# A post-norm layer (sparse attention, gated network) on one core: the down product moved into the next batch's slots, gate and up spread, a constant matrix pass taken out

## The reference, cut to what matters

```python
Q, K, V = proj(Wq, bq), proj(Wk, bk), proj(Wv, bv)          # (16, 16 heads, 512, 16)
scores = einsum('bhqd,bhkd->bhqk', Q, K) / sqrt(16)
thresh = top_k(scores, 31)[0][..., -1:]
attn = softmax(where(scores < thresh, -inf, scores))
x = layernorm(x + (attn @ V) @ Wo.T + bo)
g, u = x @ (w_gate / 127).T, x @ (w_up / 127).T              # int weights, hidden 768
x = layernorm(x + (silu(g) * u) @ (w_down / 127).T)
```

## Time and profile before

| what | value |
|---|---|
| median of 3 runs | 2992.36 us (2987.83 to 2993.67) |
| profiled execution | 3002.92 us, span 3001.1 us |
| PE busy | 2705.3 us (90%) |
| DVE busy | 2499.2 us (83%) |
| ACT busy | 2478.7 us (83%) |
| POOL busy | 2385.7 us (79%) |
| mean granted TensorE clock | 0.959 of full speed |

### The profile page before, as it was taken

One profiled execution on the slowest core, in us unless ns is written; L12 is line 12 of the kernel. 1 busy time (PEld: TensorE's weight loads), 2 busy tenths in 40 slices (PEclk: granted clock), 3 DMA queues, 4 the chain that ended last, 5 costly groups with the idle time before them and its releaser, 6 DMA issues.

```text
span 3001.1 us, 81706 instructions
## 1 busy us (share of the span) xinstructions
PE 2705.3 (90%) x21375; PEld 1449.9 (48%) x21375; DVE 2499.2 (83%) x12312; ACT 2478.7 (83%) x5890; POOL 2385.7 (79%) x1668
## 2 busy tenths in 40 slices
PE   5889999989998988899999999999988999899897
PEld 2444544545454444454545455454444545455455
DVE  5888888888889878888898988878888888888883
ACT  4888898888898877888888988878978888888883
POOL 1887888888798876787888888787877879778783
PEclk7899999999999989899999999999999999999998
DMA  3201111020111101111011110211101111110100
GB/s 88 48 21 42 25 41 38 24 49 26 37 30 36 42 21 37 29 29 45 23 42 25 41 39 24 47 27 37 30 25 45 26 40 27 32 42 23 37 2 22
DMA packets 91162, 102.67 MB, mean 34 GB/s; under 512 B 34529, under 2 KB 52962, under 8 KB 90594
## 3 DMA queue, kind: packets, MB, share of 16 engines
q1 hardware_dynamic: 89874, 96.35, 13.4%
q10 hardware_dynamic: 720, 0.14, 0.0%
HBM read 20.86 MB, written 8.39 MB: 10 GB/s over the span
## 4 chain that ended last, share of the span: by engine, by line
PE 36%; DVE 18%; SPq 15%; issue 13%; POOL 8%; ACT 6%; DMA 2%; DVEq 1%; ACTq 0%; POOLq 0%
SPq L386 8%; SPq L385 7%; DVE cand L941 7%; POOL mask L1219 6%; PE bench L740 5%; PE Y_ps L664 5%; PE ST_ps L684 4%; PE Y_ps L661 3%; PE ctxT_ps L698 3%; DVE S L934 3%; PE bench L734 3%; PE bench L605 3%; PE Y_ps L662 3%; PE ST_ps L681 3%; ACT junk L492 2%
## 5 line engine op out<-in xcount | busy, mean ns | idle before, releaser
L1219 POOL TENSOR_SCALAR mask<-S,thr,mb 128x512 bf16<-128x512 f32 x1015 | 2098.4, 2080 | 44.1 <-POOL mb L1213 33.5
L941 DVE MAX8 cand<-Y_ps 128x8 f32<-128x128 f32 x4096 | 1072.0, 282 | 7.4 <-issue 6.9
L492 ACT ACTIVATE junk<-S,at_zero,slope 128x512 bf16<-128x512 f32 x1024 | 824.7, 805 | 99.3 <-DVE S L934 99.2
L934 DVE TENSOR_SCALAR_CACHE_REDUCE S<-S_ps,na 128x512 f32<-128x512 f32 x1024 | 755.9, 738 | 170.7 <-PE S_ps L651 153.2
L502 ACT ACTIVATE above<-S,s,steep 128x512 bf16<-128x512 f32 x1024 | 824.6, 805 | 0.6
L510 ACT ACTIVATE PT<-ST_ps 128x512 f32<-128x512 f32 x1024 | 595.9, 582 | 193.0 <-PE ST_ps L684 187.4
L661 PE MATMUL Y_ps<-ones_b,nbig 128*128 128x512 bf16 x1024 | 403.0, 394 | 169.6 <-DVE cand L941 155.9
L651 PE MATMUL S_ps<-KS,QS 64*128 64x512 f32 x1024 | 523.0, 511 | 4.5 <-DVE S L934 2.3
L664 PE MATMUL Y_ps<-KS,QS 64*128 64x512 f32 x1024 | 523.0, 511 | 0.0
L684 PEld LDWEIGHTS ST_ps<-nbig,mask 128*128 128x128 bf16 x4096 | 235.8, 99 | 382.0 <-issue 382.0
L684 PE MATMUL ST_ps<-nbig,mask 128*128 128x128 bf16 x4096 | 414.8, 225 | 0.0
(11 more groups left out here) (187 smaller groups left out, 3684.6 us busy)
## 6 DMA issues: line engine op xcount, KB each, us to landing
QS<-Qhi SPq DMA_DIRECT2D x512, 32.0 KB, 2.0
KS<-Khi SPq DMA_DIRECT2D x512, 32.0 KB, 2.0
KS<-Klo SPq DMA_DIRECT2D x512, 32.0 KB, 2.0
QS<-Qlo SPq DMA_DIRECT2D x512, 32.0 KB, 2.0
xTs<-in_xT SPq DMA_DIRECT2D x17, 512.0 KB, 3.7
xs<-in_x SPq DMA_DIRECT2D x16, 512.0 KB, 3.9
out<-xs SPq DMA_DIRECT2D x15, 512.0 KB, 2.9
hT<-in_wgT SPq DMA_DIRECT2D x1, 768.0 KB
```

The costliest lines, as they stand in the source:

```text
L492: nc.scalar.activation(junk[:, :], S[:, score_place(j)[0], :], ACT.Tanh, bias=at_zero[:, :], scale=slope[:, hb, col:col + 1], accum_out=s0 ...
L934: nc.vector.tensor_scalar(S[:, at, :], S_ps[n % 2][:, :], na[:, hb, col:col + 1], None, ALU.add, op1=ALU.max, accum_out=rmax[:, n % RING:n ...
L941: mx = nc.vector.max(cand[:, j % CANDS, i, :], Y_ps[j % 2][:, i * BW:(i + 1) * BW])
L1219: nc.gpsimd.tensor_scalar(mask[:, h % MASKS, t, :], S[:, score_place(j)[0], :], thr[:, r:r + 1], mb[:, r:r + 1], ALU.is_lt, op1=ALU.add).t ...
```

## The change

- Scores are made small: the K weights and bias are multiplied once by `SHIFT` (2^-38), the exponential undoes it, `BIG` falls from 2^40 to 4.
- `count_second` writes its sign as an unsigned byte into the upper byte of each bf16 of `above` (the lower bytes stay 0). A negative sign gives 0, a positive one a tiny bf16, and one product with `nbyte` (-2^127 on the diagonal) pushes the flagged scores down. The product of `nbig` with ones (line 661) is gone.
- The flags and `onesc` are bf16.
- Gate and up move to slots 43/44, 46/47, 49/50, 52/53, 58/59, 61/62; the second half's gram, quad and sums from 36, 37, 55 to 42, 45, 54.
- The down product moves from slots 59 to 62 to slots 1, 2, 3, 5 of the next batch; the second layer norm to slot 7 on POOL, 10 and 12 on ACT.
- Batch 1, which has no down product, is unrolled; the loops start at batch 2, with 7 batches in the body for PE, ACT and POOL and 2 for DVE.

```diff
-BIG = 2.0 ** 40
+SHIFT = 2.0 ** -38
+BIG = 4.0
+BYTE_BIG = 2.0 ** 127
-             26: "v", 31: "q", 33: "k", 35: "keys", 36: "gram", 37: "quad", 55: "sums"}
+             26: "v", 31: "q", 33: "k", 35: "keys", 42: "gram", 45: "quad", 54: "sums"}
-GATE_SLOTS = {42: 0, 44: 1, 46: 2, 49: 3, 51: 4, 53: 5}
-UP_SLOTS = {43: 0, 45: 1, 47: 2, 50: 3, 52: 4, 54: 5}
-DOWN_SLOTS = {59: 0, 60: 1, 61: 2, 62: 3}
+GATE_SLOTS = {43: 0, 46: 1, 49: 2, 52: 3, 58: 4, 61: 5}
+UP_SLOTS = {44: 0, 47: 1, 50: 2, 53: 3, 59: 4, 62: 5}
+DOWN_SLOTS = {1: 0, 2: 1, 3: 2, 5: 3}
-LN_SLOTS = {34: 0, 63: 1}
+LN1_SLOT, LN2_SLOT = 34, 7
-OUT_SLOTS = {1: (0, 1), 2: (2, 3)}
+OUT_SLOTS = {10: (0, 1), 12: (2, 3)}
-        if n in DOWN_SLOTS:
-            uses.append(("down", DOWN_SLOTS[n]))
+    if finish and n in DOWN_SLOTS:
+        uses.append(("down", DOWN_SLOTS[n]))
-TURN_OF, ACT_TURN_OF = 5, 7
+TURN_OF, DVE_TURN_OF = 7, 2
-        onesc = sb("onesc", [P, 1])
+        onesc = sb("onesc", [P, 1], BF16)
-        flag = sb("flag", [P, 2, PAIR + 1])
+        flag = sb("flag", [P, 2, PAIR + 1], BF16)
...
-                nc.scalar.activation(above[:, j % 4, :], S[:, score_place(j)[0], :], ACT.Sign, bias=s0[:, j % 8:j % 8 + 1],
+                nc.scalar.activation(above[:, j % 4, :].bitcast(U8).rearrange("p (l y) -> p l y", y=2)[:, :, 1], S[:, score_place(j)[0], :], ACT.Sign, bias=s0[:, j % 8:j % 8 + 1],
...
-                nc.scalar.activation(PT[:, j % 4, :], ST_ps[j % 2][:, :], ACT.Exp, scale=SCALE).then_inc(exp_done, 1)
+                nc.scalar.activation(PT[:, j % 4, :], ST_ps[j % 2][:, :], ACT.Exp, scale=SCALE / SHIFT).then_inc(exp_done, 1)
...
-                nc.tensor.matmul(Y[:, :], nbig[:, :], ones_b[:, :], start=True, stop=False)
-                nc.tensor.matmul(Y[:, :], nbig[:, :], above[:, j % 4, :], start=False, stop=False)
+                nc.tensor.matmul(Y[:, :], nbyte[:, :], above[:, j % 4, :], start=True, stop=False)
...
-                        pe.wait_ge(h_done, b * NF)
+                        pe.wait_ge(h_done, (b - 1) * NF)
                         mm = narrow(part)
...
-            pe.wait_ge(w_loaded, 16 * N_W)
+            pe.wait_ge(consts_done, 1)
             project(1, 0, Y_ps[1]).then_inc(first_made, 1)
-            pe.wait_ge(consts_done, 1)
...
-            nc.vector.memset(ones_b[:, :], 1.0)
+            nc.vector.memset(above[:, :, :], 0.0)
...
-            nc.vector.tensor_scalar(nbig[:, :], ident[:, :], -BIG, None, ALU.mult).then_inc(consts_done, 1)
+            nc.vector.tensor_scalar(nbig[:, :], ident[:, :], -BIG, None, ALU.mult)
+            nc.vector.tensor_scalar(nbyte[:, :], ident[:, :], -BYTE_BIG, None, ALU.mult)
+            nc.vector.tensor_scalar(bqk[1][:, :], bqk[1][:, :], SHIFT, None, ALU.mult)
+            nc.vector.tensor_scalar(wqk[1][:, :, :], wqk[1][:, :, :], SHIFT, None, ALU.mult).then_inc(consts_done, 1)
...
-            with dve.Fori(1, B, TURN_OF) as b:
-                for i in range(TURN_OF):
-                    slots(b + i, False, False)
-            slots(B, False, True)
+            slots(1, False, False, False)
+            with dve.Fori(2, B, DVE_TURN_OF) as b:
+                for i in range(DVE_TURN_OF):
+                    slots(b + i, False, False, True)
+            slots(B, False, True, True)
...
-                    if not first and not rest and n in LN_SLOTS:
-                        layer_norm(b, LN_SLOTS[n])
+                    if not first and not rest and n == LN1_SLOT:
+                        layer_norm(b, 0)
+                    if finish and n == LN2_SLOT:
+                        layer_norm(b - 1, 1)
```

More of the change, by code:

```diff
@@ L44 @@
 RANKS = 16
-TINY = 1.0e-30
+TINY = 1.0e-36
 COUNT0 = 1
@@ L99, in due, with uses_of @@
     return (n >= lag and not rest) or (n < lag and not first)
-def uses_of(n, first, rest):
+def uses_of(n, first, rest, finish):
     uses = []
@@ L144, in count, with place @@
     return have
[L147 to L153, removed]
+FIRST_COUNT = count(True, False, False)
+SECOND_COUNT = count(False, False, False)
+BATCH_COUNT = count(False, False, True)
+def place(b, n, what, part, first, rest, finish):
+    have = count(first, rest, finish, (n, (what, part)))
     if first:
         return have
-    return (b - 1) * BATCH_COUNT + (FIRST_COUNT + have)
+    if not finish:
+        return FIRST_COUNT + have
+    return (b - 2) * BATCH_COUNT + (FIRST_COUNT + SECOND_COUNT + have)
 def build(nc, xT, x, wqT, wkT, wvT, woT, bq, bk, bv, bo, wgT, wuT, wdT, ident_in, blocks_in, heads_in, ranks_in, out):
@@ L398, in _, with steps @@
                     load_network()
-            def steps(b, first, last):
+            def steps(b, first, last, finish):
                 if not first:
@@ L403, in steps @@
                     load_x(b - 1)
-                wait_apart(sp, taken, place(b, KEYS_AT[0], "k", 0, first, False) + 1)
+                wait_apart(sp, taken, place(b, KEYS_AT[0], "k", 0, first, False, finish) + 1)
                 for h in range(HALF, H):
@@ L413, in steps @@
                 if not last:
-                    wait_apart(sp, taken, place(b, KEYS_AT[1], "k", 0, first, False) + 1)
+                    wait_apart(sp, taken, place(b, KEYS_AT[1], "k", 0, first, False, finish) + 1)
                     for h in range(HALF):
@@ L574, in _ @@
             slots(1, False, False, False)
-            with act.Fori(2, B, ACT_TURN_OF) as b:
-                for i in range(ACT_TURN_OF):
+            with act.Fori(2, B, TURN_OF) as b:
+                for i in range(TURN_OF):
                     slots(b + i, False, False, True)
@@ L742, in narrow, with on_bench @@
                 return mm
-            def on_bench(b, n, first, rest):
-                for what, part in uses_of(n, first, rest):
-                    use = place(b, n, what, part, first, rest)
+            def on_bench(b, n, first, rest, finish):
+                for what, part in uses_of(n, first, rest, finish):
+                    use = place(b, n, what, part, first, rest, finish)
                     pe.wait_ge(taken, use)
@@ L1061, in late_mask, with slots @@
                                         ALU.is_lt, op1=ALU.add).then_inc(mask_late, 1)
-            def slots(b, first, rest):
+            def slots(b, first, rest, finish):
                 dve.drain()
@@ L1125, in slots @@
                         if what == "down":
-                            row_statistics(b, 1, (part,), taken, use + 1)
+                            row_statistics(b - 1, 1, (part,), taken, use + 1)
                     if not first and not rest and n - 2 in OUT_PROJ:
@@ L1129, in slots @@
                         row_statistics(b, 0, (2 * part, 2 * part + 1), taken,
-                                       place(b, n - 2, "out_proj", part, first, rest) + 1)
+                                       place(b, n - 2, "out_proj", part, first, rest, finish) + 1)
                     if rest and n < MASK and (n - MASK) % 2:
@@ L1248, in slots @@
                         cut(b, T, n, first)
-                    for what, part in uses_of(n - 1, first, rest) if n else []:
+                    for what, part in uses_of(n - 1, first, rest, finish) if n else []:
                         if what == "up":
-                            use = place(b, n - 1, "up", part, first, rest)
+                            use = place(b, n - 1, "up", part, first, rest, finish)
                             pool.wait_ge(taken, use + 1)
```

55 lines of the change are left out of this document (30 added, 25 removed).

## The result

The changed kernel takes **3075.3 us** (3067.96 to 3081.97, 4 runs), the kernel before 2992.2 beside it (2987.83 to 2993.67). The ratio is 1.028, 95% interval 1.0254 to 1.0305. Forecast were 3008 us, range 2948 to 3045: slower, as the likeliest case said, but by 83 us and not by 16, and outside the range.

What follows compares the result with a forecast made beforehand. A different engine or chain was taken to bound each stretch: PE, ACT, SP's transfers, ACT and POOL in plain slots. From the profiled 3003: -30 stretches, +36 loops, +2 PE's branch, +8 clock = 3019, or 3008 against the 2992.4 median; range 2948 to 3045.

Steps and rivals of the forecast that it cites:

- the clock: Whole run: a lighter PE brings a third more time at the lower clock, 80 us; +8 us, range 0 to +40.
- the case: Clock rival: the lower level spreads through slots 14-30 and 0-5, 3043 us; chance 0.07.
- Slots 14-30: SP's chain of transfers sets 46.9 us whatever the engines do; 0.2 us a batch lost, nothing gained.
- the sum over the stretches: Six slot stretches of a batch together: -2.0 us a batch, -30 us over 15; bounds -93 to +16.
- branches of DVE and PE: Loop ends: DVE's six branches back instead of two, +36 us, and PE's moved branch, +2 us.
- Slots 42-54: Eight of twelve gate and up products stay, POOL becomes longest with 32.2 us; 4.2 us a batch gained from 36.4.
- Slots 0-5: They get the four down products, PE setting the pace: 22.5 us from 14.4, 8.1 us a batch lost.
- The collision with the statistics: Slots 55-63: second-half statistics share slots with DVE's threshold choice; 1.6 us a batch added, 3.7 if whole.
- Branches: DVE's loop: each of six branches back costs 8.2 us, against two at 6.8 before; +35.6 us, range +5 to +39.
- PE's branch: PE's loop branch of 3.4 us, no longer behind queued down products, after slot 63: +2 us, 0 to +3.6.
- POOL's race in slot 1: The down product waits for POOL's last product of slot 63: 4.0 us against 4.1, just fits; otherwise 13 us.
- The faster rival: More of PE's 14 us a batch comes through, 5.5 us a batch gained, 2955 us; chance 0.38.

Runs made afterwards that it cites:

- experiment 4: The changed kernel with seven batches in DVE's loop body instead of two, so one branch back instead of six: 3037.3 us, ratio 1.0144.
- experiment 6: The changed kernel with the byte product issued twice in every slot (PE's old work) and seven batches in DVE's body: 3037.1 us, ratio 1.0141.
- experiment 3: The kernel before with the byte flags alone, one product instead of two, old slots and old loops: 3016.2 us, ratio 1.0052.
- 11: The kernel of experiment 5 with its spare products at 256 columns instead of 512: 2973.5 us, ratio 0.9943.
- experiment 5: The kernel of experiment 3 plus a second, overwritten product of 512 columns in slots that PE does not pace: 2964.3 us, ratio 0.9905.
- 2: The changed kernel with the byte product issued a second time in slots 14 to 30 alone: 3050.6 us, ratio 1.0196.

## Why the prediction was wrong

**The step that failed is the clock**, "+8, range 0 to +40". Mechanism and direction were there, and the case was given 0.07; its size was not. It was reasoned that a third more low time would come, 80 us, and that little of it is lost where others set the pace. The second half held, the first did not. The runs show three times as much low time, 738 us where 246 were. What such time costs is seen between experiments 4 and 6, which differ by the pass alone: 320 us more of it in slots 14-41 and 55-63 cost 43 us, an eighth, and the forecast had taken a tenth. So +8 measured about +43.

Where a fall does cost, the rows of slots 17 to 19 show how: they took 1.8 to 2.1 us and take 2.5 to 3.2, because PE at the lower level is slower than the engines that paced them. Part of it is made up later in the stretch. The earlier trace rows had a warning: in slots 14-30 PE was busy 41.83 of 47.4 us at full clock, so products half as long again make it the bound.

**The second step that failed is the sum over the stretches**, -30 us. By the experiments the +83 us split so:

| part | forecast | by experiments |
|---|---|---|
| stretches and ends, clock held | -30 | about +10: new slots +51 (6), removed pass -41 (4 against 6) |
| branches of DVE and PE | +38 | about +32: 38 for five (4), 7.6 for the sixth, less 13.6 for the two of before |
| clock | +8 | about +43 (4 against 6) |

Each part is known to some 10 us; the profiled execution of before alone lies 10.6 us over its median. The +10 us are about what came on top behind the last batch, 11 us, which the forecast had put at nothing. The down product of a batch now stands in slots of the next one, so batch 1 has none, and the slots that drain the pipeline hold four (48 products of 128x256, 11.3 us of PE's time). The stretch from slot 0 behind the last batch to the end, before and then after:

```profile
2920.30:3001.10 80.80, 60.11 (x478) 40.60 (x477) 30.42 (x105) 30.33 (x57) 31.26 (x30) 0.90 0.07 21
```

```profile
2981.60:3073.60 92.00, 71.64 (x520) 50.50 (x520) 34.01 (x117) 31.33 (x61) 34.14 (x32) 0.90 0.06 18
```

In the batches themselves the new slots and the removed pass come out at about nothing, where -2.0 us a batch were forecast. Slots 42-54 take 1.5 us more than forecast though their clock is near full. In experiment 6, whose low time (283 us) is near that of before, slots 14-30, 31-41 and 55-63 reach their forecasts only in batches where they have none of it (46.7 to 47.9, 28.7 to 30.3 and 23.4 us) and are 1 to 2 us longer in the median; slots 6-13 are shorter than forecast. The direction rested on the branches, and that term held.

That a fuller PE moves the time is shown in the series 3, 11, 5 and by 2 against the changed kernel; the ten runs of 3 go along with it. What makes the clock fall at slot 24 or 58 and not elsewhere is not shown.

The Trainium skill (TensorE: Matmul & The Clock Gate, "What's actually happening") was cited for a throttled default that activity lifts; this case agrees, with clocks of 0.896, 0.934 and 0.956 as PE's spare work grows (3, 11, 5). Its section "A second HAM failure mode: psum-queue depth-cycling" tells of a PE whose frequent short pauses between groups of products let the clock swing. Pauses of 0.27 and 1.38 us in slot 15 ahead of a fall are in line with it; that they cause the fall, no run shows.

The other steps:
- **Slots 0-5**, 22.5: 22.7. Moving the down product buys nothing, as said.
- **Slots 6-13**, 20.5: 18.2. The normalisations hide; 2.3 better.
- **Slots 14-30**, 47.6: 51.3, the clock; at a held clock still 48.6 to 48.8 (2, 6), of which the stall in slot 15 is 0.7 to 0.9. That stall the forecast did not have.
- **Slots 31-41**, 29.0: 30.1 (30.5 before). The quad's wait is still there, only moved to slot 46: line 742 waits for it 11.9 us in 15 batches, against 17.2.
- **Slots 42-54**, 32.2: 33.7. In batch 11 POOL is busy 32.18 of 33.4 us, the engine that was named. These slots keep a clock near full, so the 1.5 us over the forecast are not the clock's.
- **Slots 55-63**, 23.2: 25.4. The collision with the statistics is there. Waits of the weight loads of line 742 (gate and up), total, times, longest:

```profile
PEld bench L742 <- DVE th L1104: 47.4, 60, 7.8
...
PEld bench L742 <- DVE ctxs L1043: 34.8, 15, 3.0
...
PEld bench L742 <- DVE quad L898: 11.9, 15, 1.5
```

The largest of these waits was not in the forecast: four times a batch, the product that follows a gate product waits until DVE has emptied the bank, 47.4 us in all where it was 11.3 (line 734). The gate product of slot 58 waits 2.3 us a batch for a copy that stands on DVE behind the statistics, and 13 falls of the clock stand in that slot. In experiment 6 the batches without low time take 23.0 to 23.4 us there, which is the forecast; the median is 25.3.
- **Branches**, 8.2 each: 5.5 in slots 0-5, 7.6 by experiment 4. The changed kernel has six. Timeline of DVE at the first of them:

```profile
729.49 0.08 DVE L942 DVE_READ_ACCUMULATOR S<-S_ps,na 128x1 f32 x1
731.95 0.29 DVE L998 TENSOR_REDUCE least<-picked 128x8 f32<-128x128 f32 x1 [2.38 <-issue]
732.27 0.82 DVE L1000 SCALAR_TENSOR_TENSOR flag<-hidden,least 128x8 bf16<-128x8 f32 x1
```

One stall of 2.38 us (2.29 to 2.43 at the six) where 3.60 and 1.58 stood, and two instructions of 0.82 and 0.79 us where 0.17 and 0.16 are usual (as in batch 11). The rest comes behind it: the clock is 0.88 in that stretch. The Trainium skill (Runtime: NRT & Kernel Launch, "Instruction fetch mechanics") has it that a taken branch to a target outside the pages held stalls; this trace agrees, with those stalls on DVE.
- **PE's branch**, +2 (0 to +3.6): slots 62 and 63 of batch 8, where it stands, take 10.1 us and 4.4 in others, so it costs 5.7.
- **Byte output**, 0: 808 ns beside 805 for bf16. **POOL's race in slot 1**: not seen; no product of line 748 is recorded as waiting for POOL.

The faster rival failed with the clock: it asked for 5.5 us a batch, and experiment 5, with a held clock and old slots, brings about 2.

## What to carry to other kernels

Before taking work off TensorE in slots that another engine paces, price one such slot at 1.2 GHz: if PE would then be the slower, the removal can cost more than it saves, and a spare product in the same slots may be worth its place (here 44 to 52 us of 3016). Compare such kernels by granted clock and time together. And move a product only out of a stretch that PE sets into one that it does not; between two that it sets, it costs the same and brings its waits along. If it moves into the next turn of a pipeline, count what it adds behind the last one (here 11 us).

## What the runs showed of the hardware

- Ten runs of one program (experiment 3) spread over 33 us, and the granted clock fell from 0.913 to 0.896 roughly as the time rose.
- Low time was cheap where other engines pace: 320 us of it cost 43 us (4 against 6), and in experiment 3 another 96 us of it in slots 14-30 left their median 0.3 us longer.
- Spare products of 0, 256 and 512 columns in 35 of 64 slots gave clocks of 0.896, 0.934 and 0.956; a second one in slots 22-25 gave nothing more.
- A busy PE did not bring the clock back at once. From slot 17 to 22 of the changed kernel's batch 11 it stays at 0.50, though PE is busy nearly all of that time:

```profile
2096.45:2115.17 18.72, 18.25 (x108) 9.97 (x110) 15.15 (x78) 14.59 (x37) 16.27 (x10) 0.50 0.24 52
```

- ScalarE's write of bytes two apart costs what its write of bf16 does, 808 and 805 ns.
